# First feed-forward product in seven block products per pair of feature tiles, with the second product woven between them

## The reference, cut to what matters

```
n = layernorm(x + attention)                        # 896 x 1024, its transpose is kept as "x2"
h = relu(n @ up_w) ** 2                             # up_w 1024 x 2048
shared = h @ down_w                                 # down_w 2048 x 1024
routed = ((n @ fc1_w @ expert_w) * route) @ fc2_w   # route: sum of the two largest of 8 gate logits
out = x + attention + layernorm(shared + routed) * gamma + beta
```

## Time and profile before

| what | us |
|---|---|
| median of 3 runs (1762.29 to 1765.58) | 1763.38 |
| profiled execution, its own time | 1766.59 |
| its span in the trace | 1764.8 |
| PE busy | 1743.3 (99%) |
| DVE busy | 886.4 (50%) |
| POOL busy | 875.5 (50%) |
| ACT busy | 663.9 (38%) |

### The profile page before, as it was taken

One profiled execution on the slowest core, in us unless ns is written; L12 is line 12 of the kernel. 1 busy time (PEld: TensorE's weight loads), 2 busy tenths in 40 slices (PEclk: granted clock), 3 DMA queues, 4 the chain that ended last, 5 costly groups with the idle time before them and its releaser, 6 DMA issues.

```text
span 1764.8 us, 24917 instructions
## 1 busy us (share of the span) xinstructions
PE 1743.3 (99%) x8709; PEld 1532.0 (87%) x8709; DVE 886.4 (50%) x1426; ACT 663.9 (38%) x1298; POOL 875.5 (50%) x714
## 2 busy tenths in 40 slices
PE   9999999999999999999999999999999999999997
PEld 8988998889999988888988898889888988888886
DVE  3521112633434357865777577767565222353257
ACT  3221212233334357634773477257412213212310
POOL 2546452235555548875767576635534222222226
PEclk9999999999999999999999999999999999999999
DMA  9878886256767668844763576334212112111113
GB/s 281 262 258 291 277 285 214 90 179 204 222 218 250 214 208 280 293 125 143 252 206 118 171 239 202 119 104 147 84 68 100 60 54 90 59 56 53 57 51 131
DMA packets 194259, 296.26 MB, mean 168 GB/s; under 512 B 18960, under 2 KB 158480, under 8 KB 193296
## 3 DMA queue, kind: packets, MB, share of 16 engines
q1 hardware_dynamic: 194192, 295.41, 51.6%
HBM read 197.10 MB, written 98.27 MB: 167 GB/s over the span
## 4 chain that ended last, share of the span: by engine, by line
PE 88%; DMA 5%; POOL 2%; issue 2%; DVE 1%; SPq 1%; ACT 0%; POOLq 0%; DVEq 0%; ACTq 0%
PE bank L1685 28%; PE bank L1686 27%; PE bank L1687 27%; PE bank L1902 5%; DMA weight_sums_scratch<-slab_raw 1%; POOL slab_raw L797 1%; DMA slab_raw<-in_slabs 1%; DMA tile_region<-in_ctxT 1%; DMA slab_raw<-in_wkv 1%; DMA k_ctx_scratch<-small_region 1%; DMA mid_region<-k_latents_scratch 0%; PE bank L2024 0%; PE bank L1728 0%; DMA small_region_unrounded<-in_slabs 0%; PE bank L1757 0%
## 5 line engine op out<-in xcount | busy, mean ns | idle before, releaser
L833 POOL TENSOR_TENSOR tile_region<-tile_region,small 128x487 f32<-128x487 f32 x224 | 220.9, 1023 | 69.7 <-DVE small L1374 69.7
L1685 PE MATMUL bank<-mid_region 125*128 125x448 f32 (+4 forms) x596 | 242.6, 407 | 1.0 <-DVE mid_region L1429 0.5
L1687 PE MATMUL bank<-mid_region 125*128 125x448 f32 (+4 forms) x596 | 222.9, 374 | 0.0
L1686 PE MATMUL bank<-mid_region 128*128 128x488 f32 (+4 forms) x560 | 209.3, 374 | 0.0
L1063 ACT ACTIVATE tile_region<-bank,small 128x487 f32<-128x487 f32 x224 | 153.6, 686 | 29.8 <-DVE small L1378 29.8
L1095 ACT ACTIVATE mid_region<-bank 125x512 fp32r<-125x512 f32 x224 | 136.6, 612 | 58.2 <-PE bank L1902 58.2
L1378 DVE TENSOR_REDUCE small<-bank 128x1 f32<-128x487 f32 x224 | 145.9, 652 | 24.9 <-PE bank L1687 24.9
L1429 DVE TENSOR_TENSOR mid_region<-bank,mid_region 125x512 fp32r<-125x512 f32 x224 | 151.6, 682 | 8.2 <-ACT mid_region L1095 8.2
L817 POOL TENSOR_TENSOR slab_split<-slab_raw,slab_split 128x512 fp32r<-128x512 f32 x64 | 87.2, 1366 | 129.3 <-ACT slab_split L1018 129.3
L1685 PE MATMUL bank<-mid_region,act_region 128*125 128x512 f32 (+2 forms) x384 | 151.4, 394 | 0.0
L1687 PE MATMUL bank<-mid_region,act_region 128*125 128x512 f32 (+2 forms) x384 | 151.0, 393 | 0.0
(11 more groups left out here) (204 smaller groups left out, 4072.3 us busy)
## 6 DMA issues: line engine op xcount, KB each, us to landing
slab_raw<-in_slabs SPq DMA_DIRECT2D x68, 512.0 KB, 3.5
q_scratch<-y_region SPq DMA_DIRECT2D x16, 1792.0 KB, 8.1
mid_region<-q_scratch SPq DMA_DIRECT2D x32, 896.0 KB, 6.9
slab_raw<-in_slabs SPq DMA_DIRECT2D x80, 256.0 KB, 4.1
weight_sums_scratch<-slab_raw SPq DMA_DIRECT2D x32, 512.0 KB, 5.0
v_scratch<-slab_split SPq DMA_DIRECT2D x8, 1536.0 KB, 7.8
slab_raw<-weight_sums_scratch SPq DMA_DIRECT2D x48, 256.0 KB, 4.7
mid_region<-v_scratch SPq DMA_DIRECT2D x32, 384.0 KB, 3.2
```

What stands on the lines that cost most here:

```text
L833: pool.tensor_tensor(PR[i][:, 0:KEYS], PR[i][:, 0:KEYS], rrow[:, i:i + 1].broadcast_to([P, KEYS]), ALU.mult).then_inc(s_pn, 1)
L1685: pe.matmul(out_ap, w[0], a[0], start=first, stop=False)
L1686: pe.matmul(out_ap, w[0], a[1], start=False, stop=False)
L1687: return pe.matmul(out_ap, w[1], a[0], start=False, stop=last)
```

## The change: what it does

The up product goes by Strassen's scheme in Winograd's form. Pair p takes feature tiles 2p and 2p+1; the 896 rows are cut into halves of 448 and the 1024 inputs into halves of 512. Seven products n = 0 to 6, each of 12 matmuls with 448 columns, give the four result blocks. There are 8 pairs.

- Row sums T2, T3, T1 and T4 of x2 (1792 columns each) are formed by DVE in nine steps, rounded by ACT and completed by DVE during fc1, exp and fc2; the last (T4) at the start of the new stage.
- Each pair loads four raw weight blocks (A11, A12, A21, A22) of 512 columns. POOL forms four sums in place (`up_sum`), ACT rounds each of the seven blocks (`up_hi`), and POOL completes it (`up_lo`). There are two unit buffers, F_UNIT, so block u+2 is rounded after product u has ended.
- DVE combines the products; four results per pair are squared (ACT relu, DVE square, ACT hi, DVE lo).
- The down product of pair p is 14 groups of 6 matmuls with 512 columns, woven two by two behind the seven up products of pair p+1, for p = 0 to 5. Pairs 6 and 7 follow together as 14 groups of 12, in the order DOWN_LAST. Down slabs go through one raw buffer, DOWN_RAW: `load_down`, then `down_hi` on ACT, `down_lo` on POOL.
- The up products use the four banks GB, the down products four others. The first four up products each wait for the last SEG2 group evicted from their bank.
- In attention, `late` now covers i = 0, 1 and 2.

The diff, cut to its core (SP, POOL, ACT, DVE and PE in this order):

```diff
+F_PAIRS = INT // (2 * P)
+F_BLOCKS = ("A11", "S2", "A12", "S3", "S1", "A22", "S4")
+F_TILES = {2: (0, 0), 4: (1, 1), 5: (1, 0), 6: (0, 1)}
+F_SUMS = ("T2", "T3", "T1", "T4")
...
+DOWN = [(r, eh) for eh in range(2) for r in range(RT)]
+DOWN_LAST = [(0, 0), (1, 0), (0, 1), (1, 1)] + [(r, eh) for r in range(2, RT) for eh in range(2)]
...
+        F_ROWS = {"A11": F11, "S2": F_T2, "A12": F21, "S3": F_T3, "S1": F12, "A22": F_T4, "S4": F22}
...
+        HID_T = [[part(t, at + l * 2 * ROWS, 2 * ROWS).rearrange("p (m n) -> p m n", m=2) for l in range(2)]
+                 for t, at in ((RA, 6 * F_WORDS), (RC, 0))]
+        F_UNIT = [[part(RA, 2 * NK * ROWS + l * 512, 512) for l in range(2)], [part(RC, 4 * ROWS, 512), part(FB_R, 4 * ROWS, 512)]]
+        F_FIRST, F_U = [part(YR, RT * HID + i * HALF, HALF) for i in range(2)]
+        F_TMP = [[part(t, i * HALF, HALF) for i in range(4)] for t in (RC_RAW, FB)]
+        DOWN_RAW = part(FB, 4 * HALF, SLAB)
+        F_BLOCK = {f"A{i + 1}{j + 1}": part(RAW, (2 * i + j) * 512, 512) for i in range(2) for j in range(2)}
...
+            def load_down(d):
+                p, eh = d // 2, d % 2
+                sp.wait_ge(s_dlo, d)
...
+            sp.wait_ge(s_wlo, P_FFN)
+            for name in ("A11", "A21", "A22", "A12"):
+                load_up(0, name)
+            for p in range(F_PAIRS):
+                more = p + 1 < F_PAIRS
+                if more:
+                    sp.wait_ge(s_ulo, 7 * p + 4)
+                    load_up(p + 1, "A11")
+                if p > 0:
+                    load_down(2 * p)
+                if more:
+                    for n, name in ((4, "A21"), (5, "A22"), (6, "A12")):
+                        sp.wait_ge(s_ulo, 7 * p + n + 1)
+                        load_up(p + 1, name)
+                if p == 0:
+                    sp.wait_ge(s_ftlo, 4)
+                    load_down(0)
+                load_down(2 * p + 1)
             sp.wait_ge(s_x2st, 16 * RT)
-            sp.wait_ge(s_ev, C_SEG2 + SEG2.index(("logitT", 0)) + 1)
+            sp.wait_ge(s_up, 7 * (F_PAIRS - 1) + 5)
             sp.dma_start(GAMMA, gamma.partition_broadcast(P)).then_inc(s_gamma, 16)
-            for r in range(2):
+            for r in range(3):
...
-                    late = kv == 0 and i < 2
+                    late = kv == 0 and i < 3
...
-                        output_sums(kv, i, 0)
+                        output_sums(kv, i % 2, i // 2)
...
+            def up_sum(step, p, out, a, b, op):
+                if step == 1:
+                    for name in ("A21", "A22"):
+                        pool.wait_ge(s_ur[name], 16 * (p + 1))
+                else:
+                    pool.wait_ge(s_usum, 4 * p + step - 1)
+                pool.tensor_tensor(F_BLOCK[out], F_BLOCK[a], F_BLOCK[b], op).then_inc(s_usum, 1)
+            def up_lo(p, n):
+                u = 7 * p + n
+                pool.wait_ge(s_uhi, u + 1)
+                pool.tensor_tensor(F_UNIT[u % 2][1], F_BLOCK[F_SRC[F_BLOCKS[n]]], f32(F_UNIT[u % 2][0]), ALU.subtract).then_inc(s_ulo, 1)
+                if n in (0, 2):
+                    pool.wait_ge(s_ulo, u + 1)
+            def down_lo(d):
+                pool.wait_ge(s_dhi, d + 1)
+                pool.tensor_tensor(down_slot(d)[1], DOWN_RAW, f32(down_slot(d)[0]), ALU.subtract).then_inc(s_dlo, 1)
+            for p in range(F_PAIRS):
+                last = p == F_PAIRS - 1
+                up_sum(1, p, "A21", "A21", "A22", ALU.add)
+                up_lo(p, 0)
+                up_sum(2, p, "A11", "A21", "A11", ALU.subtract)
+                up_lo(p, 1)
+                up_lo(p, 2)
+                up_sum(3, p, "A12", "A12", "A11", ALU.subtract)
+                up_sum(4, p, "A11", "A22", "A11", ALU.subtract)
+                up_lo(p, 3)
+                if p > 0:
+                    down_lo(2 * p - 1)
+                up_lo(p, 4)
+                if last:
+                    down_lo(2 * p)
+                up_lo(p, 5)
+                up_lo(p, 6)
+                if not last:
+                    down_lo(2 * p)
+            down_lo(2 * F_PAIRS - 1)
...
+            def up_hi(p, n):
+                u, name = 7 * p + n, F_BLOCKS[n]
+                if name[0] == "A":
+                    act.wait_ge(s_ur[name], 16 * (p + 1))
+                else:
+                    act.wait_ge(s_usum, 4 * p + {"S1": 1, "S2": 2, "S4": 3, "S3": 4}[name])
+                if u >= 2:
+                    act.wait_ge(s_up, u - 1)
+                act.activation(F_UNIT[u % 2][0], F_BLOCK[F_SRC[name]], ACT.Copy).then_inc(s_uhi, 1)
+            def down_hi(d, freed=None):
+                act.wait_ge(s_draw, 16 * (d + 1))
+                if freed is not None:
+                    act.wait_ge(s_mm, freed)
+                act.activation(down_slot(d)[0], DOWN_RAW, ACT.Copy).then_inc(s_dhi, 1)
+            def hidden_hi(p, n, i):
+                m, h = F_TILES[n]
+                src_, relu, sq = (F_FIRST, *F_TMP[p > 0][2:4]) if n == 2 else F_TMP[p > 0][1:4]
+                act.wait_ge(s_upc, 7 * p + {2: 2, 4: 4, 5: 6, 6: 7}[n])
+                if p > 0 or i > 0:
+                    act.wait_ge(s_sq, 4 * p + i)
+                act.activation(relu, src_, ACT.Relu).then_inc(s_relu, 1)
+                act.wait_ge(s_sq, 4 * p + i + 1)
+                if p >= 2:
+                    act.wait_ge(s_mm, down_done(p - 2, len(DOWN)))
+                act.activation(HID_T[p % 2][0][:, m, h * HALF:(h + 1) * HALF], sq, ACT.Copy).then_inc(s_hhi, 1)
...
+            act.wait_ge(s_mm, C_FFN)
+            up_hi(0, 1)
+            row_block_hi("T4", 9)
+            for p in range(F_PAIRS):
+                last = p == F_PAIRS - 1
+                for n in range(7):
+                    if n == 0:
+                        act.wait_ge(s_up, 7 * p + 1)
+                        act.activation(F_FIRST, GB[0][:, 0:HALF], ACT.Copy).then_inc(s_first_p, 1)
+                    if n < 5 or not last:
+                        up_hi(p + (n >= 5), (n + 2) % 7)
+                    if n in F_TILES:
+                        hidden_hi(p, n, list(F_TILES).index(n))
+                    if n == 1 and p > 0:
+                        down_hi(2 * p - 1, down_done(p - 1, 0) if p > 1 else None)
+                    if n == 2 and last:
+                        act.wait_ge(s_up, 7 * p + 2)
+                        down_hi(2 * p)
+                    if n == 4 and not last:
+                        down_hi(2 * p, down_done(p - 1, RT) if p > 0 else None)
+            act.wait_ge(s_up, 7 * F_PAIRS - 3)
+            down_hi(2 * F_PAIRS - 1)
...
+            ROW_BLOCK_STEPS = {("fc1", 1, 0): (0,), ("fc1", 2, 0): (1,), ("fc1", 3, 0): (2,), ("exp", 1, 0): (3,), ("exp", 2, 0): (4,),
+                               ("fc2", 0, 0): ("T2",), ("fc2", 1, 0): ("T3",), ("fc2", 2, 0): (5,), ("fc2", 4, 0): (6,),
+                               ("fc2", 5, 0): ("T1",), ("fc2", 6, 0): (7,), ("fc2", 1, 1): (8,)}
...
+            def hidden_square(p, n, i):
+                src_, relu, sq = (F_FIRST, *F_TMP[p > 0][2:4]) if n == 2 else F_TMP[p > 0][1:4]
+                dve.wait_ge(s_relu, 4 * p + i + 1)
+                if p > 0 or i > 0:
+                    dve.wait_ge(s_hlo, 4 * p + i)
+                dve.scalar_tensor_tensor(out=sq, in0=src_, scalar=0.0, in1=relu, op0=ALU.max, op1=ALU.mult).then_inc(s_sq, 1)
+            def hidden_lo(p, n, i):
+                m, h = F_TILES[n]
+                x = [t[:, m, h * HALF:(h + 1) * HALF] for t in HID_T[p % 2]]
+                dve.wait_ge(s_hhi, 4 * p + i + 1)
+                dve.tensor_tensor(x[1], F_TMP[p > 0][3], f32(x[0]), ALU.subtract).then_inc(s_hlo, 1)
+            for p in range(F_PAIRS):
+                U3_, OUT_ = F_TMP[p > 0][0:2]
+                for n in range(7):
+                    if n == 1:
+                        dve.wait_ge(s_first_p, p + 1)
+                        up_combine(p, 1, n, F_U, F_FIRST, ALU.add)
+                        if p == 0:
+                            row_block_step("T4")
+                    if n == 2:
+                        up_combine(p, 2, n, F_FIRST, F_FIRST, ALU.add)
+                    if n == 3:
+                        up_combine(p, 3, n, U3_, F_U, ALU.add)
+                    if n == 4:
+                        up_combine(p, 4, n, OUT_, U3_, ALU.add)
+                        up_combine(p, 5, n, F_U, F_U, ALU.add)
+                    if n >= 5:
+                        dve.wait_ge(s_sq, 4 * p + n - 3)
+                    if n == 5:
+                        up_combine(p, 6, n, OUT_, U3_, ALU.subtract)
+                    if n == 6:
+                        up_combine(p, 7, n, OUT_, F_U, ALU.add)
+                    for i in range(2):
+                        if 1 <= p < F_PAIRS - 1:
+                            j = 2 * n + i
+                            add_down(C_FFN + len(DOWN) * (p - 1) + j, *DOWN[j])
+                        if n in F_TILES:
```

(37 more changed lines are left out.)

216 lines of the change are left out of this document (118 added, 98 removed).

## The result

Before 1765.58 us median (5 runs), changed 1774.03 (5 runs): ratio 1.0054, 95% interval [1.0038, 1.0069]. A second set of five gave 1774.10 against 1765.10 (17 runs), 1.0050 [1.0036, 1.0063]. The kernel before came out 2 us above the 1763.38 of the three first runs; the difference is 8.5 to 9.0, forecast was 6.0. The measured 1774.0 lies inside the range of 1760 to 1777 and just above the forecast's own range of 1766 to 1773. The profiled execution took 1772.06, its span 1770.3.

A forecast was written before the change was run, and what follows sets the result against it. PE, busy 99% of the span, was taken as the bound. -18.5 - 1.3 + 1.0 + 0.25 + 4.3 + 8.8 + 2.1 + 9.35 = +6.0 on 1763.4 gave 1769.4 us; range 1760 to 1777, own range 1766 to 1773.

The forecast's parts named there:

- PE's work: Feed-forward up products: seven products of 448 columns per pair take 136.2 us instead of 154.7, gain 18.5 us.
- Start of the stage: First up product wants bank 0, which the last SEG2 group still holds until its eviction; cost 1.0 us.
- Pair 0's fourth product: Product 3 of pair 0 waits for POOL's sums and lo, lengthened by turns with DVE's T4 step; 4.3 us.
- rival 2: POOL and DVE do not take turns in the narrow stretches: waits 3.9 less, 1765.5 us, no measurable change; chance 0.20.
- The seam: From pair 0 to pair 1, ACT, POOL and PE are stuck behind down slab 0's load; PE idle 8.8 us.
- Pair 7: Last up pair, nothing woven: products 2, 3, 4 and 5 late by 0.25, 2.3, 1.9 and 4.9, together 9.35 us.
- product 4 late by 1.9: In pair 7, POOL does slab 13's lo and, after a square's turn, lo 4, so product 4 starts 1.9 us late.
- product 5: In pair 7, slab 14's load, hi and lo stand ahead of block 5's hi and lo; product 5 late by 4.9.
- Attention: Moved sums remove PE's 2.93 us wait at 686; 1.6 comes back at the next batch, gain 1.3 us.
- The clock: Only the 8.8 us wait drops PE's clock, the 4.3 and 4.9 leave it at full; coming back costs 2.1 us.
- Rival 1: The clock falls in all three long waits, two more returns at 2.1 each: 1773.6 us; chance 0.16.
- Rival 3: Faster: the seam behind pair 0 costs nothing, so 8.8 and 2.1 go: 1758.5 us; chance 0.16.

The follow-up runs named there:

- Banks one further: Changed kernel with up product n in bank (n + 1) % 4 instead of n % 4: 1772.9 us, ratio to the kernel before 1.0050.
- T4's move: Changed kernel with DVE's low half of row sum T4 ahead of the first combine instead of behind it: 1772.5 us, ratio to the kernel before 1.0037.
- slab 14 early: Changed kernel with pair 7's first down slab loaded earlier into room of its own, its lo behind the sixth product's: 1768.4 us, ratio to the kernel before 1.0021.
- the filled kernel: Changed kernel with 78 matmuls on data that nothing reads in PE's four longest waits: 1769.0 us, ratio to the kernel before 1.0025.
- the four moves: Changed kernel with T4's remainder ahead, slab 0 loaded and split inside pair 0, slab 14 loaded early, and banks one further: 1761.9 us, ratio to before 0.9985.
- slab 0 first: Kernel with the four moves, pair 0's first down slab load also moved ahead of the next pair's A11 load: 1756.6 us, ratio to the kernel before 0.9948.

## Why the prediction was right, and which steps were off

The direction, the size within the range, and the place of every wait came out. The size is in part luck: the sum had two errors of opposite sign (waits 3.3 too long, slow clock 5.5 too short), and the clock's was the larger.

- *PE's work, -18.5.* Right: 36.17 a pair, no wait in pairs 1 to 6.
- *Start of the stage, 1.0.* Measured 1.01 (0.84 idle). Banks one further took this wait away, but no gain in time is shown for it.
- *Pair 0's fourth product, 4.3.* 3.9. T4's move shows the two parts, 2.3 for the sums and 1.6 for the turns (2.0 forecast), against rival 2.
- *The seam, 8.8.* 8.2 here, 9.0 in the second set. The mechanism is shown by two runs: the load three places earlier takes 3.0 off, hi and lo out of the queue the rest. The prediction put the landing (20.5) 4.0 behind lo 6 (16.5), though its row gives 3.5 for a load; measured from the end of lo 6 (1463.85) to ACT's start (1467.85) it is 4.0, since SP issues A12's load first.
- *Pair 7, 9.35.* 0.35 + 2.15 + 0.4 + 4.15 = 7.05. Of the missing 2.3, 1.5 were not saved but covered: "product 4 late by 1.9" came as 0.4 of waiting and 1.4 of slow matmuls. The other 0.8 is product 5, late by 4.15 and not 4.9: each link of that chain was a little shorter than put down (slab 14's lo ended 16.7 behind product 0, not 17.1, and lo 5 at 18.3, not 19.05). The slab's part is shown by slab 14 early.
- *Attention, -1.3.* 2.1 by the trace, 2.8 by the runs. Forecast was 1.6 of waiting at the next batch, measured 0.7 to 0.9; the moved sums began 0.8 earlier than forecast, since the load that POOL's first four sums wait for had landed earlier.
- *The clock, 2.1: the step that failed.* The words were "the wait of 8.8 should drop it, and I leave the two of 4.3 and 4.9 at full". It fell after both, and after one of 2.15 as well; 7.6 by the account, 5.1 by the filled kernel. The Trainium skill's advice against such gaps ("TensorE: Matmul & The Clock Gate", section "Why this matters for your kernels") was the better guide for the three long waits: this trace agrees, with 0.50 granted behind each. It does not cover the fall behind the wait of 2.15, which is shorter than the gaps it warns of. Rival 1, all three waits cold, gave 1773.6. That this is nearly the measured 1774.0 is luck: it stood on a kernel before of 1763.4, which came out at 1765.6. As differences it said 10.2, the forecast 6.0, and 8.5 to 9.0 was measured. I had set five microseconds at full behind the last matmul against it. Those rows show when the clock falls, not which wait makes it fall: here it fell at 1456.1, 4.7 us after PE ran dry and 1.0 after it had work again.

Rival 3's condition, that the slab's landing "would have to be 8 us earlier", points the right way: with the load 15 us earlier (issued at 1448.80 against 1464.30), and its hi and lo inside pair 0, the seam costs 0.6 to 0.8. With slab 14 early as well 1756.6 was reached, where the prediction had named 1749 for no wait at the seam or in pair 7; 2.0 and 1.3 of waiting are left in pair 7, and 2.1 in pair 0.

Against the forecast of 6.0: waits 20.4 for 23.7, -3.3; clock +5.5; attention -0.8 to -1.5; pace and the open rest +1.1. That gives 7.8 to 8.5; measured 8.5 to 9.0.

## What to carry to other kernels

An interleaving that hides a chain covers only its middle: cost its first and last rounds by themselves, instruction by instruction through each in-order queue, since here 20 us of waits and some 5 of low clock ate a saving of 18.5. Put a load where its buffer comes free, not where the code that uses it stands: one queue position was worth 3.5 us of the stage here (5.3 in the runs). When a mended chain is composed with others, look at the next timeline; a slow clock can lie over a wait and hide it. And compare each with the kernel before of its own set: a shift of 0.9 us, counted three times, made most of the theory's error for the four moves.

## What the runs showed of the hardware

- **The same wait does not always bring the clock down.** A wait of 2.09 ahead of pair 0's fourth product, in the four-moves kernel and then with slab 0 first (windows 1453 to 1455, 1455 to 1459):

```profile
1453.00:1455.00 2.00, 0.06 (x1) 1.00 0.00 0
1455.00:1459.00 4.00, 4.00 (x20) 1.00 0.75 258
```
```profile
1453.00:1455.00 2.00, 0.19 (x1) 1.00 0.00 0
1455.00:1459.00 4.00, 4.00 (x13) 0.57 0.37 131
```
  The waits have the same length and the same 0.70 of idle time ahead of the product before; 20 matmuls started in four microseconds, or 13. In the kernel before, 2.93 left it at 1.00. So did 2.09 with T4's remainder early, and the 1.98 ahead of pair 7's fourth product with the four moves, which brought the clock down in the changed kernel. What decides between them was not tried.
- **A fall outlasts its wait.** In the changed kernel PE worked for 3.5, 5.3, 3.0 and 3.5 us at 0.50 after the four waits, and lost half of that, also after the wait of 1.98.
- **A slow clock costs little where the next product waits anyway**: filling two such waits in the fastest kernel won 0.2 us in the runs, less than its interval, and 0.7 by the stage, where the two stretches had taken some 3.3 us each at half clock.
- **The same load lands late at times**: from issue to ACT's first use slab 0 took 3.5 to 3.6 us in three executions, 4.3 in one and 4.8 in one, and the seam's wait moved with it.
- **The turns that POOL and DVE take reach short instructions too**: a square of 0.63 took 1.88 and 2.21 next to POOL's 2.34 and 2.39 on a slab. I had used this for T4's 1792 columns and left rival 2 a chance of 0.20 for the short ones.
